# First attention of a hybrid block: one product for the narrow scores, and the next sequence's projections moved within the loop

## The chip, the cores and the metric

The kernel runs on one core of a Trainium2 chip. The metric is the device time of one execution in microseconds. TensorE (PE in the profile) multiplies and transposes, PEld are its weight loads, VectorE is DVE, ScalarE is ACT, GpSimd is POOL, and SyncE (SP) issues the DMAs.

## The reference

A batch of 16 sequences of 512 tokens and width 256 goes through four layers with residuals: attention A, a feed-forward layer with FP4 weights, attention B, and the feed-forward layer again. The change touches attention A and the preparation of weights behind it. Cut to what matters:

```python
q, k, v = split_heads(x @ Wq.T), split_heads(x @ Wk.T), split_heads(x @ Wv.T)   # 16 heads of 16, x normalised
scores = einsum('bhqd,bhkd->bhqk', q, k) * hd ** -0.5
stride = 22                                                                   # int(sqrt(512))
strided = causal & ((i - j < stride) | (j % stride == i % stride))            # heads 0 to 7
fixed = causal & ((j // stride == i // stride) | (j % stride >= stride - 1))  # heads 8 to 15
attn = softmax(where(head_mask, scores, neg_inf))
x = x + (attn @ v) @ Wo.T
```

With the fixed mask a tile of 128 queries needs few keys: its own 128, the 32 before it, and each 22nd key of the whole row (16 "far" columns).

## The kernel before

`attention_a` computes one sequence after another. A sequence has 16 groups n of four heads: `group(n)` gives the half c (0: strided heads, the wide half; 1: fixed heads), the tile t of 128 queries and the parity e. Groups 0 to 7 are wide, with 128, 256, 384 and 512 keys (two groups of each), groups 8 and 9 have 128 keys, groups 10 to 15 are narrow with 176 keys: 16 far and 160 near.

The loop over n is a pipeline that each engine goes through in an order written out by hand. In slot n, for each of the four heads j, TensorE computes the score (`score_head`), transposes the probabilities of group n-1 (`turn_head`, into one of two banks that VectorE and ScalarE empty by turns in `move_turned`), and weighs the values of group n-2 (`weigh`) behind the second head. VectorE masks and takes the maximum (`mask_max`, line 330), ScalarE takes the exponential (`exps`, line 409). A score of head j waits for the maximum of the same head in the group before, since there is one score bank a head.

Beside this, TensorE does one "side job" at the end of some slots (`a_side_jobs`), all in the one PSUM bank `side`: xT0 and xT1 turn the next sequence's normalised input, Q0, K0, V0 and Q1, K1, V1 are its projections for each half, R0 and R1 turn the reciprocal sums, y0 and y1 are the output projection of the sequence before. The result is moved away in slot n+1. xT and V go behind the second head, on one engine. For Q and K ScalarE writes a high part behind the second head (line 396) and VectorE the low part behind the third (line 304), both into `part`; TensorE's next side job waits for the semaphore `s_free` that this gives. SyncE then places the parts with six DMAs for each of Q and K (`place`, line 222) into `stack_q` and `stack_k`, from which the scores are read. `part` is shared by both halves, so ScalarE waits before the high part of one half until all twelve DMAs of the other half have landed:

```python
wait(act, s_placed[1 - c], 192 * (c if s is None else s + 1 + c))
```

The DMAs of half 1 wait for the third group's scores of the next sequence, as `stack_k` of that half is read until then.

Behind the attention, `prepare` quantises three weight matrices in blocks and turns them (`scales`, `mark`, `turn`, `move`), folds the small matrices of attention B (`fold_heads`, `fold_up`, `fold_down`) and runs the first normalised input of the feed-forward layer through its front, all in an order fixed by hand on each engine.

Of the kernel before, what the change touches and what calls it, by code (L numbers as in the profile page):

```python
# [4 lines left out]
FP32 = mybir.dt.float32  # L5
FP16 = mybir.dt.float16
FP32R = mybir.dt.float32r
# [29 lines left out]
A_FAR = 16  # L37
A_REST = A_FAR + A_NEAR
A_NARROW = A_REST + P
A_SIDE_FRONT = ["xT0", "xT1", "Q0", "K0", "V0", "Q1", "K1"]  # L40


# [3 lines left out]
def a_side_jobs(kind):  # L46


    jobs = {}
    if kind != "first":  # L50
        jobs |= {0: "R1", 2: "y0", 3: "y1"}
    if kind != "tail":
        jobs |= {1: "V1", 8: "R0"}
        if kind != "last":
            jobs |= {4: "xT0", 5: "xT1", 6: "Q0", 7: "K0", 9: "V0", 11: "Q1", 13: "K1"}
    return jobs, [jobs[n] for n in sorted(jobs)]


# [12 lines left out]
def attention_a(nc, s_passed, xs, ident, consts, x_in, w_q, w_k, w_v, w_o, masks):  # L71
    front = len(A_SIDE_FRONT)
    ctx = ExitStack()
    with ctx:
# [19 lines left out]
        xT = sb("xT", [P, KC, SEQ])  # L94


        part = sb("part", [P, 2, 2, SEQ], FP32R)
        stack_q = sb("stack_q", [P, 2, 2, 4, SEQ], FP32R)
        stack_k = sb("stack_k", [P, 2, 4, SEQ], FP32R)
        vb = sb("vb", [P, 2, TILES, 4, 64])  # L100
        v_rest = sb("v_rest", [P, TILES - 1, 4, 64])
        probs = sb("probs", [P, 2, 4, SEQ])
# [51 lines left out]
        def chunk(n, row, u):  # L154
# [2 lines left out]
                return row[:, u * P:(u + 1) * P]  # L157
            return row[:, 0:A_REST] if u else row[:, A_REST:A_NARROW]

        def mask_of(n):  # L160
            c, t, _ = group(n)
            if c == 0:
                return mask[:, SEQ - keys(n):SEQ]
            at = SEQ + (P + (t - 1) * A_NARROW if t else 0)
            return mask[:, at:at + keys(n)]
# [32 lines left out]
        def _(sp):  # L198
# [11 lines left out]
            def place(s, job):  # L210

                i, c = "QK".index(job[0]), int(job[1])
                sp.wait_ge(s_free, job_index(s, order_of(s), job) + 1)
                sp.sem_inc(s_passed, 1)
                if s is not None:
                    sp.wait_ge(s_score, 64 * s + (32, 64 + A_AFTER_SWITCH)[c])
                for b, h in enumerate(((0, 0, 1), (0, 1, 0))[i]):
                    for e in range(2):
                        frm = part[64 * e:64 * e + 64, i, h, :].bitcast(FP32)
                        at = slice(64 * e + 16 * b, 64 * e + 16 * b + 16)  # L220
                        to = stack_k[at, c, :, :] if i else stack_q[at, e, c, :, :]
                        sp.dma_start(to.bitcast(FP32), frm).then_inc(s_placed[c], 16)

            def place_all(s):
# [18 lines left out]
            for dst, src in ((wq, w_q), (wk, w_k), (wv, w_v), (wo, w_o), (mask, masks)):  # L243
                sp.dma_start(dst[:], src).then_inc(s_w, 16)
            load(1)
            sp.wait_ge(s_zero, 4)
            place_all(None)
            load(2)
            place_rest(0)
# [9 lines left out]
        @block.gpsimd  # L259
        def _(pool):  # L260
            pool.memset(vb[:], 0.0).then_inc(s_zero, 1)
            pool.memset(stack_q[:].bitcast(FP32), 0.0).then_inc(s_zero, 1)
            pool.memset(stack_k[:].bitcast(FP32), 0.0).then_inc(s_zero, 1)
            pool.memset(v_rest[:], 0.0).then_inc(s_zero, 1)

            def rstd_of(s):
                pool.wait_ge(s_var, s + 1)
                pool.tensor_tensor(out=rstd[:], in0=vare[:], in1=consts[:, 0:TILES],  # L268
                                   op=ALU.pow).then_inc(s_rstd, 1)

            rstd_of(0)
            for s in range(1, SEQS):
                rstd_of(s)

        @block.vector
        def _(dve):
# [20 lines left out]
            def move_side(s, order, job):  # L297
                k = job_index(s, order, job)
                dve.wait_ge(s_job, k + 1)
                c = int(job[-1])  # L300
                if job[0] in "QK":
                    i = "QK".index(job[0])
                    dve.wait_ge(s_hi, parts_before(s, job) + 1)
                    dve.scalar_tensor_tensor(out=part[:, i, 1, :], in0=side[:], scalar=(0.25, 1.0)[i],
                                             in1=part[:, i, 0, :], op0=ALU.mult, op1=ALU.subtract).then_inc(s_free, 1)
                elif job[0] == "V":
                    if s is None and c == 0:
                        dve.wait_ge(s_zero, 1)
                    src = side[:].rearrange("p (a e d) -> p a e d", e=2, d=16)
                    for e in range(2):  # L310
                        dst = vb[:, c, :, :, :].rearrange("p t j d -> p (t j) d")[:, :, 48 * e:48 * e + 16]
                        m = dve.tensor_copy(dst, src[:, :, e, :])
                    m.then_inc(s_free, 1)
                elif job == "xT1":
                    dve.tensor_copy(xT[:, 1, :], side[:]).then_inc(s_free, 1)
                else:
                    for a in range(2):
                        x = x_tile(xs, s - 1, 2 * c + a)
                        m = dve.tensor_tensor(out=x, in0=side[:, a * H:(a + 1) * H], in1=x, op=ALU.add)
                        if a == 1:  # L320
                            m.then_inc(s_free, 1)
# [64 lines left out]
        def _(act):  # L386
            def move_side(s, order, job):
# [5 lines left out]
                elif job[0] in "QK":  # L393
                    i = "QK".index(job[0])
                    wait(act, s_placed[1 - c], 192 * (c if s is None else s + 1 + c))
                    act.activation(part[:, i, 0, :], side[:], ACT.Copy, scale=(0.25, 1.0)[i]).then_inc(s_hi, 1)
                else:
                    s = sequence(s, job)
                    wait(act, s_o, s * 2 + c)
                    act.activation(rsb[:], side[:], ACT.Copy).then_inc(s_rsb, 1)  # L400
                    act.wait_ge(s_rsb, s * 2 + c + 1)
                    act.sem_inc(s_free, 1)
# [35 lines left out]
        def _(pe):  # L438
# [34 lines left out]
            def score_head(s, n, j):  # L473
# [4 lines left out]
                    pe.wait_ge(s_placed[c], 192 * (s + 1))  # L478
                q = stack_q[0:112, e, c, j, t * P:(t + 1) * P]
                if narrow(n):  # L480
                    far = slice(A_STRIDE - 1, A_STRIDE * A_FAR, A_STRIDE)
                    mm(score[j][:, 0:A_FAR], q, stack_k[0:112, c, j, far], start=True, stop=True)
                    m = mm(score[j][:, A_FAR:A_NARROW], q, stack_k[0:112, c, j, t * P - A_NEAR:(t + 1) * P],
                           start=True, stop=True)
                else:
                    m = mm(score[j][:, 0:keys(n)], q, stack_k[0:112, c, j, 0:keys(n)], start=True, stop=True)  # L486
                m.then_inc(s_score, 1)

            def turn_head(s, n, j):
# [82 lines left out]
def prepare(nc, ident, wguT, wdT, a, w, front):  # L572
# [5 lines left out]
    with ctx:  # L578
# [39 lines left out]
        row1 = pb("row1", [P, H])  # L618

        s_raw = [sem("loaded_" + n) for n, *_ in items]  # L620
        s_w = sem("second_attention_loaded")
        s_v = sem("scale_steps")
        s_inv = sem("inverse_ready")
# [14 lines left out]
                    turns.append((m, k, half))  # L638
        for c in range(IC):
            turns.append((2, c, 0))  # L640
        loads = [(wqT, "b_wqT"), (wkT, "b_wkT"), (c2q, "b_c2q"), (bq, "b_bq"), (bk, "b_bk"), (bv, "b_bv"), (bc, "b_bc"),
                 (w1T, "b_w1T"), (wm, "b_wm"), (b1, "b_b1"), (bm, "b_bm"), (wqoT, "b_wqoT"), (bqo, "b_bqo"),
                 (w2, "b_w2"), (wq_in, "b_wq"), (bq_in, "b_bq_turned"), (w["bk"], "b_bk_turned"), (w["wk"], "b_wk"),
                 (w["wv"], "b_wv"), (w["wo"], "b_wo"), (w["rows"], "b_rows"), (w["sum8"], "b_sum8")]

        def shape(i):
            _, p, f, _ = items[i]
# [4 lines left out]
        @block.sync  # L652
        def _(sp):
            for (n, p, f, src), dst, s in zip(items, raw, s_raw):
                sp.dma_start(dst[:], src).then_inc(s, 16)
            for dst, name in loads:
                sp.dma_start(dst[:], a[name]).then_inc(s_w, 16)

        @block.gpsimd
        def _(pool):  # L660
# [13 lines left out]
            front.pool_norm(pool, 0)  # L674
            divide(0)
            divide(1)
            front.pool_divide(pool, 0)
            scale(0)
            pool.wait_ge(s_deq, 2)
            divide(2)  # L680
            scale(1)
            front.pool_scale(pool, 0)
            scale(2)

        @block.vector
        def _(dve):
# [35 lines left out]
            front.vector_norm(dve, 0)  # L722
            scales(0)
            scales(1)
            front.vector_scales(dve, 0)
            mark(0)
            scales(2)
            mark(1)
            front.vector_round(dve, 0)
            for n in range(4):  # L730
                move(n)
            mark(2)
            dve.wait_ge(s_deq, 1)
            for n in range(4, len(turns)):
                move(n)
            dve.wait_ge(s_w, 16 * len(loads))
            dve.tensor_scalar(out=w["wq"][:], in0=wq_in[:], scalar1=CW_SCALE, scalar2=None, op0=ALU.mult)
            dve.tensor_scalar(out=w["bq"][:], in0=bq_in[:], scalar1=CW_SCALE, scalar2=None, op0=ALU.mult)
# [11 lines left out]
        def _(act):  # L750
# [12 lines left out]

            front.scalar_standard(act, 0)
            magnitude(0)
            front.scalar_magnitude(act, 0)
            magnitude(1)
            magnitude(2)
            for n in range(8):
                high(n)  # L770

        @block.tensor
        def _(pe):
# [41 lines left out]
                    m = mm(row2[:], bqo[:, n:n + 1].to_broadcast([P, P]), w2[:, n, :], start=n == 0, stop=n == FC - 1)  # L815
                m.then_inc(s_mm, 1)

            pe.wait_ge(s_w, 16 * len(loads))
            fold_heads()
            for n in range(4):  # L820
                turn(n)
            fold_up()
            for n in range(4, 8):
                turn(n)
            fold_down()
            for n in range(8, len(turns)):
                turn(n)


class XFront:  # L830
# [1328 lines left out]
```

## Time and profile before

| | |
|---|---|
| median of 3 runs | 3564.15 us (3558.09 to 3564.78) |
| profiled execution | 3559.97 us, span in the trace 3558.2 us |
| attention A | from 3.6 us (first memset) to 1060 us |
| preparation | 1060.3 to 1132.9 us |
| a sequence of attention A | 63.2 us |
| busy: PE, DVE, ACT, POOL | 3088.3, 2790.0, 2184.9, 1121.6 us |

Times in the rows are microseconds from the start of the span. "128x176 f32" is partitions by elements. In a row of the timeline the bracket says how long the engine stood idle before it and what released it.

### The profile page before, as it was taken

How to read it: one execution, taken by the hardware profiler on the slowest of the kernel's cores; microseconds unless marked ns; L12 is line 12 of the kernel's file. 1: busy time of each engine (PE TensorE's matmuls, PEld its weight loads, DVE VectorE, ACT ScalarE, POOL GpSimd, SP SyncE). 2: the span in 40 equal slices, each digit the busy share in tenths (PEclk: the TensorE clock that was granted, in tenths of full speed). 3: DMA queues.
4: the chain of work that ended last, by engine and by line, in shares of the span. 5: the costliest groups of instructions: out<-in, count | busy, mean ns of one | idle time of the engine just before them, and what ended most of it. 6: DMA issues, size and time to landing. Idle time of an engine off the chain costs nothing. (4 is left out here: it accounts for less than half of the span.)

```text
span 3558.2 us, 70567 instructions
## 1 busy us (share of the span) xinstructions
PE 3088.3 (87%) x24024; PEld 2396.3 (67%) x24024; DVE 2790.0 (78%) x7209; ACT 2184.9 (61%) x5360; POOL 1121.6 (32%) x664
## 2 busy tenths in 40 slices
PE   6999999999985999995888888888888886799998
PEld 4666666666664888884556556656655654688888
DVE  4776777767767999993778888888888887699997
ACT  3777777777762343432777877777777775344443
POOL 1000000000004555553123444433333333455554
PEclk9999999999996999997898989989999997899999
DMA  4344443434422000001344444334434433111000
GB/s 90 46 70 62 62 71 45 70 62 63 63 37 102 13 19 19 19 19 30 48 61 69 62 72 72 60 60 67 72 60 67 71 54 89 42 36 32 29 30 24
DMA packets 134182, 190.46 MB, mean 54 GB/s; under 512 B 15126, under 2 KB 81558, under 8 KB 133142
## 3 DMA queue, kind: packets, MB, share of 16 engines
q1 hardware_dynamic: 133830, 185.95, 30.3%
q8 instruction: 199, 3.26, 0.4%
q14 instruction: 153, 1.25, 0.2%
HBM read 45.65 MB, written 28.84 MB: 21 GB/s over the span
## 5 line engine op out<-in xcount | busy, mean ns | idle before, releaser
L409 ACT ACTIVATE a_probs<-a_probs,a_negmax 128x176 f32<-128x176 f32 (+4 forms) x1024 | 502.6, 491 | 265.7 <-DVE a_negmax L330 259.8
L330 DVE CUSTOM_DVE_ANT_0 a_probs<-a_mask,a_score 128x176 f32<-128x176 f32 (+4 forms) x1024 | 404.1, 401 | 270.5 <-PE a_score L486 114.4
L1718 DVE CUSTOM_DVE_ANT_0 b_u<-b_u,b_score 128x512 f32<-128x512 f32 x512 | 340.8, 682 | 135.3 <-PE b_score L1973 132.8
L494 PE MATMUL a_turned<-ident,a_probs 128*128 128x128 f32 (+1 forms) x2176 | 411.4, 280 | 37.7 <-DVE a_pT L339 29.7
L1843 ACT ACTIVATE b_u<-b_u,b_negmax 128x512 f32<-128x512 f32 x512 | 367.1, 717 | 112.0 <-DVE b_negmax L1718 110.4
L1247 PE MATMUL f_y_bank<-f_wdT,f_hqT 128*128 128x256 f32 x1536 | 357.0, 382 | 40.6 <-ACT f_hqT L1186 36.9
L1710 DVE SCALAR_TENSOR_TENSOR b_u<-b_u,b_score 128x1024 f32<-128x1024 f32 x256 | 310.0, 1215 | 93.5 <-ACT b_u L1836 91.1
L1836 ACT ACTIVATE b_u<-b_score 128x1024 f32<-128x1024 f32 x256 | 262.0, 1024 | 162.3 <-PE b_score L1963 161.9
L1247 PEld LDWEIGHTS f_y_bank<-f_wdT,f_hqT 128*128 128x128 f32 x1536 | 284.6, 190 | 89.5 <-issue 56.4
L1982 PE MATMUL b_turned<-ident,b_u 128*128 128x128 f32 x2048 | 320.6, 281 | 24.9 <-DVE b_pT L1724 19.5
L1982 PEld LDWEIGHTS b_turned<-ident,b_u 128*128 128x128 f32 x2048 | 248.6, 145 | 97.1 <-issue 59.9
L1179 ACT ACTIVATE f_h_mag<-f_hu 128x704 f32<-128x704 f32 x128 | 100.9, 788 | 342.7 <-POOL f_hu L1062 342.7
L1070 POOL TENSOR_TENSOR f_hq<-f_h_mark,f_nscale 128x704 f32<-128x704 f32 x128 | 177.6, 1388 | 404.3 <-DVE f_h_mark L1128 404.3
L268 POOL TENSOR_TENSOR a_rstd<-a_vare,consts 128x4 f32<-128x4 f32 x16 | 16.1, 1008 | 908.7 <-DVE a_vare L286 908.6
L494 PEld LDWEIGHTS a_turned<-ident,a_probs 128*128 128x128 f32 (+1 forms) x2176 | 236.4, 134 | 94.5 <-issue 51.7
L1973 PE MATMUL b_score<-b_stack 96*128 96x512 f32 x512 | 272.1, 546 | 20.1 <-DVE b_u L1710 20.0
L1230 PE MATMUL f_gate<-f_wguT,f_xqT 128*128 128x352 f32 x1536 | 283.6, 334 | 0.0
L1230 PE MATMUL f_up<-f_wguT,f_xqT 128*128 128x352 f32 x1536 | 277.3, 329 | 0.0
L486 PE MATMUL a_score<-a_stack_k,a_stack_q 112*128 112x128 f32 (+3 forms) x640 | 248.8, 403 | 1.1 <-DVE a_negmax L330 1.1
L1230 PEld LDWEIGHTS f_gate<-f_wguT,f_xqT 128*128 128x128 f32 x1536 | 249.5, 193 | 0.1
L1230 PEld LDWEIGHTS f_up<-f_wguT,f_xqT 128*128 128x128 f32 x1536 | 244.6, 189 | 0.0
L339 DVE COPY a_pT<-a_turned 128x256 f32<-128x256 f32 (+3 forms) x512 | 224.0, 438 | 4.9 <-PE a_turned L494 1.1
(236 smaller groups left out, 7132.1 us busy)
## 6 DMA issues: line engine op xcount, KB each, us to landing
b_stack<-b_part SPq DMA_DIRECT2D x192, 256.0 KB, 8.2
a_stack_q<-a_part SPq DMA_DIRECT2D x192, 128.0 KB, 4.3
a_stack_k<-a_part SPq DMA_DIRECT2D x192, 128.0 KB, 5.3
xs<-in_x_dram SPq DMA_DIRECT2D x16, 512.0 KB, 8.5
x_before_b<-xs SPq DMA_DIRECT2D x16, 512.0 KB, 2.9
b_xin<-x_before_b SPq DMA_DIRECT2D x16, 512.0 KB, 12.2
b_xres<-x_before_b SPq DMA_DIRECT2D x16, 512.0 KB, 3.9
x_after_b<-b_xres SPq DMA_DIRECT2D x16, 512.0 KB, 5.8
```

What stands on the lines that cost most here:

```text
L330: dve.tensor_tensor_reduce(out=probs[:, n % 2, j, 0:keys(n)], in0=mask_of(n), in1=score[j][:, 0:keys(n)], scale=-1.0, scalar=3.0e38, op0=A ...
L409: act.activation(probs[:, n % 2, j, 0:keys(n)], probs[:, n % 2, j, 0:keys(n)], ACT.Exp, bias=negmax[:, n, j:j + 1], scale=-1.0, accum_out= ...
L486: m = mm(score[j][:, 0:keys(n)], q, stack_k[0:112, c, j, 0:keys(n)], start=True, stop=True)
L494: m = nc.tensor.transpose(turned[j % 2][0:rows, u, :], chunk(n, probs[:, n % 2, j, :], u), ident[:])
L1230: m = mm(dst[:, a, 0:HALF], xqT[:, i, k, t * P:(t + 1) * P], wguT[:, j, k, at:at + HALF], start=p == 0, stop=p == len(products) - 1)
L1247: m = mm(y_bank[:, 0:H], hqT[:, t % 2, c * P:(c + 1) * P], wdT[:, c, :], start=c == 0, stop=c == IC - 1)
L1710: dve.scalar_tensor_tensor(out=u[:, g, d, :], in0=u[:, g, d, :], scalar=10.0, in1=score[:, d, :], op0=ALU.add, op1=ALU.mult).then_inc(s_u, 1)
L1718: dve.tensor_tensor_reduce(out=u[:, n, j, :], in0=u[:, n, j, :], in1=score[:, j, :], scale=-0.05, scalar=3.0e38, op0=ALU.add, op1=ALU.min, ...
L1836: act.activation(u[:, g, d, :], score[:, d, :], ACT.Sin, scale=PI_IN).then_inc(s_sin, 1)
L1843: act.activation(u[:, n, j, :], u[:, n, j, :], ACT.Exp, bias=negmax[:, n, j:j + 1], scale=-1.0, accum_out=sums[:, c, t, j:j + 1]).then_inc ...
L1973: mm(score[:, j, :], stack[0:96, 0, c, j, t * P:(t + 1) * P], stack[0:96, 1, c, j, :], start=True, stop=True).then_inc(s_score, 1)
L1982: m = nc.tensor.transpose(turned[j % 2][:, t, :], u[:, n, j, t * P:(t + 1) * P], ident[:])
```

## The change

Three things are changed. The narrow score becomes one product of 176 columns instead of one of 16 and one of 160: K1's parts are laid out with 176 columns for each of the three narrow tiles (`A_WIDE` = 656 columns), by copying the far and near columns as they are moved out of the bank (three pieces on ScalarE and three on VectorE), and `stack_k` of half 1 becomes `wide_k`. The side jobs xT0, xT1, Q0, K0, V0 and Q1 move from slots 4, 5, 6, 7, 9 and 11 to 6, 7, 9, 10, 11 and 12; K1 stays in 13, R0 in 8. In `prepare` the loads of the heads' fold get their own semaphore and come first, and the orders of all engines are changed: the first input's scales and rounding come behind the weights, `fold_down` behind all turns.

```diff
+A_WIDE = P + (TILES - 1) * A_NARROW
...
-            jobs |= {4: "xT0", 5: "xT1", 6: "Q0", 7: "K0", 9: "V0", 11: "Q1", 13: "K1"}
+            jobs |= {6: "xT0", 7: "xT1", 9: "Q0", 10: "K0", 11: "V0", 12: "Q1", 13: "K1"}
...
-        part = sb("part", [P, 2, 2, SEQ], FP32R)
+        part = sb("part", [P, 2, 2, A_WIDE], FP32R)
-        stack_k = sb("stack_k", [P, 2, 4, SEQ], FP32R)
+        stack_k = sb("stack_k", [P, 4, SEQ], FP32R)
+        wide_k = sb("wide_k", [P, 4, A_WIDE], FP32R)
...
+        def part_pieces(job, row):
+            if job != "K1":
+                return [row[:, 0:SEQ]]
+            blocks = row[:, P:A_WIDE].rearrange("p (t w) -> p t w", w=A_NARROW)
+            return [row[:, 0:P], blocks[:, :, 0:A_FAR], blocks[:, :, A_FAR:A_NARROW]]
+        def side_pieces(job):
+            if job != "K1":
+                return [side[:]]
+            far = side[:, A_STRIDE - 1:A_STRIDE * A_FAR:A_STRIDE].unsqueeze(1).to_broadcast([P, TILES - 1, A_FAR])
+            return [side[:, 0:P], far, near_columns()]
...
-                        to = stack_k[at, c, :, :] if i else stack_q[at, e, c, :, :]
+                        to = (wide_k if c else stack_k)[at, :, :] if i else stack_q[at, e, c, :, :]
...
+            pool.memset(wide_k[:].bitcast(FP32), 0.0).then_inc(s_zero, 1)
...
-                    act.activation(part[:, i, 0, :], side[:], ACT.Copy, scale=(0.25, 1.0)[i]).then_inc(s_hi, 1)
+                    for high, src in zip(part_pieces(job, part[:, i, 0, :]), side_pieces(job)):
+                        m = act.activation(high, src, ACT.Copy, scale=(0.25, 1.0)[i])
+                    m.then_inc(s_hi, 1)
...
-                    far = slice(A_STRIDE - 1, A_STRIDE * A_FAR, A_STRIDE)
-                    mm(score[j][:, 0:A_FAR], q, stack_k[0:112, c, j, far], start=True, stop=True)
-                    m = mm(score[j][:, A_FAR:A_NARROW], q, stack_k[0:112, c, j, t * P - A_NEAR:(t + 1) * P],
+                    at = P + (t - 1) * A_NARROW
+                    m = mm(score[j][:, 0:A_NARROW], q, wide_k[0:112, j, at:at + A_NARROW], start=True, stop=True)
...
             front.vector_norm(dve, 0)
             scales(0)
             scales(1)
-            front.vector_scales(dve, 0)
             mark(0)
             scales(2)
             mark(1)
-            front.vector_round(dve, 0)
             for n in range(4):
                 move(n)
             mark(2)
+            front.vector_scales(dve, 0)
+            for n in range(4, 8):
+                move(n)
             dve.wait_ge(s_deq, 1)
-            for n in range(4, len(turns)):
+            for n in range(8, len(turns)):
                 move(n)
+            front.vector_round(dve, 0)
...
-            pe.wait_ge(s_w, 16 * len(loads))
+            pe.wait_ge(s_heads, 16 * len(head_loads))
             fold_heads()
             for n in range(4):
                 turn(n)
+            pe.wait_ge(s_w, 16 * len(loads))
             fold_up()
-            for n in range(4, 8):
+            for n in range(4, len(turns)):
                 turn(n)
             fold_down()
-            for n in range(8, len(turns)):
-                turn(n)
```

VectorE's low part is cut into the same pieces. In the other engines' orders of `prepare`, GpSimd's division and scaling of the first input move behind the third matrix, and ScalarE writes high parts between the magnitudes.

## Rows read from the trace of the kernel before

**Rows 1.** The page, busy time (share of the span) and instructions of each engine

```profile
PE 3088.3 (87%) x24024; PEld 2396.3 (67%) x24024; DVE 2790.0 (78%) x7209; ACT 2184.9 (61%) x5360; POOL 1121.6 (32%) x664
```

**Rows 2.** Timeline of TensorE's products in sequence 3: start, duration, instruction

```profile
249.28 0.53 PE L486 MATMUL a_score<-a_stack_k,a_stack_q 112*128 112x384 f32 x1
...
250.94 0.45 PE L486 MATMUL a_score<-a_stack_k,a_stack_q 112*128 112x384 f32 x1
...
266.62 1.98 PE L453 MATMUL a_side<-a_xT,a_wk 128*128 128x512 f32 x4 [1.05 <-DVE a_part L304]
...
274.73 0.33 PE L486 MATMUL a_score<-a_stack_k,a_stack_q 112*128 112x128 f32 x1
...
277.47 0.26 PE L482 MATMUL a_score<-a_stack_k,a_stack_q 112*128 112x16 f32 x1
...
283.67 0.58 PE L482 MATMUL a_score<-a_stack_k,a_stack_q 112*128 112x16 f32 x1
...
290.75 0.58 PE L482 MATMUL a_score<-a_stack_k,a_stack_q 112*128 112x16 f32 x1
...
291.49 0.26 PE L482 MATMUL a_score<-a_stack_k,a_stack_q 112*128 112x16 f32 x1
291.60 0.33 PE L483 MATMUL a_score<-a_stack_k,a_stack_q 112*128 112x160 f32 x1
291.76 0.39 PE L494 MATMUL a_turned<-ident,a_probs 128*128 128x128 f32 x2
...
296.44 0.31 PE L486 MATMUL a_score<-a_stack_k,a_stack_q 112*128 112x128 f32 x1
```

**Rows 3.** Timeline of TensorE in sequence 15, the last

```profile
1010.09 0.45 PE L486 MATMUL a_score<-a_stack_k,a_stack_q 112*128 112x384 f32 x1
...
1029.53 0.33 PE L486 MATMUL a_score<-a_stack_k,a_stack_q 112*128 112x128 f32 x1
...
1032.69 0.26 PE L482 MATMUL a_score<-a_stack_k,a_stack_q 112*128 112x16 f32 x1
...
1040.49 0.26 PE L482 MATMUL a_score<-a_stack_k,a_stack_q 112*128 112x16 f32 x1
```

**Rows 4.** Groups by line and shape, 0 to 1100 us: busy, mean ns | idle before

```profile
L453 PE MATMUL a_side<-a_xT,a_wk 128*128 128x512 f32 x128 | 65.3, 635 | 23.6 <-DVE a_part L304 23.6
L339 DVE COPY a_pT<-a_turned 128x128 f32<-128x128 f32 x128 | 36.7, 287 | 0.1
L462 PE MATMUL a_side<-ident,a_rec 128*128 128x128 f32 x128 | 20.0, 279 | 13.2 <-DVE a_part L304 13.2
```

**Rows 5.** Timelines of ScalarE and VectorE in slot 12 of sequence 3

```profile
286.15 0.58 ACT L396 ACTIVATE a_part<-a_side 128x512 fp32r<-128x512 f32 x1
...
286.84 0.69 DVE L304 SCALAR_TENSOR_TENSOR a_part<-a_side,a_part 128x512 fp32r<-128x512 f32 x1
```

**Rows 6.** Timeline at the start of the attention, before the first scores

```profile
26.25 3.88 SPq L222 DMA_DIRECT2D a_stack_q<-a_part  x6
...
31.31 3.75 SPq L222 DMA_DIRECT2D a_stack_k<-a_part  x6
...
41.02 0.60 ACT L396 ACTIVATE a_part<-a_side 128x512 fp32r<-128x512 f32 x1 [10.60 <-DMA a_stack_k<-a_part]
```

**Rows 7.** Timelines of VectorE and TensorE in the preparation

```profile
1097.58 1.21 DVE L921 SCALAR_TENSOR_TENSOR f_x_mark<-f_x_mag,f_xu 128x1024 f32<-128x1024 f32 x1
1098.82 4.58 DVE L924 SCALAR_TENSOR_TENSOR f_x_mark<-f_x_mag,f_x_mark 128x1024 f32<-128x1024 f32 x1
...
1103.99 1.41 PE L783 MATMUL w_bank<-ident,w_raw_gate 88*128 88x88 f32 x8 [11.69 <-DVE f_wguT L716]
...
1123.71 3.72 PE L815 MATMUL w_row<-w_w,w_bqo 128*128 128x256 f32 x16
```

**Rows 8.** Windows: busy of each engine in a stretch, granted clock, DMA share, GB/s

```profile
236.00:299.00 63.00, 58.20 (x577) 43.38 (x576) 45.64 (x192) 46.36 (x167) 1.01 (x1) 1.00 0.41 62
...
1033.00:1035.00 2.00, 1.99 (x15) 1.15 (x14) 1.39 (x8) 1.76 (x9) 0.00 (x0) 0.50 0.03 8
```

More of the change, by code:

```diff
@@ L158, in chunk, with near_columns @@
             return row[:, 0:A_REST] if u else row[:, A_REST:A_NARROW]
+        def part_pieces(job, row):
[8 more added lines that the diff above has]
+            return [side[:, 0:P], far, near_columns()]
+        def near_columns():
+            near = side[:, P - A_NEAR:2 * P]
+            return bass.AP(near.tensor, near.offset, [list(near.ap[0]), [P, TILES - 1], [1, P + A_NEAR]])
         def mask_of(n):
@@ L218, in place @@
                     for e in range(2):
-                        frm = part[64 * e:64 * e + 64, i, h, :].bitcast(FP32)
+                        frm = part[64 * e:64 * e + 64, i, h, 0:(A_WIDE if job == "K1" else SEQ)].bitcast(FP32)
                         at = slice(64 * e + 16 * b, 64 * e + 16 * b + 16)
-                        to = stack_k[at, c, :, :] if i else stack_q[at, e, c, :, :]
+                        to = (wide_k if c else stack_k)[at, :, :] if i else stack_q[at, e, c, :, :]
                         sp.dma_start(to.bitcast(FP32), frm).then_inc(s_placed[c], 16)
@@ L245, in _ @@
             load(1)
-            sp.wait_ge(s_zero, 4)
+            sp.wait_ge(s_zero, 5)
             place_all(None)
@@ L303, in move_side @@
                     dve.wait_ge(s_hi, parts_before(s, job) + 1)
-                    dve.scalar_tensor_tensor(out=part[:, i, 1, :], in0=side[:], scalar=(0.25, 1.0)[i],
-                                             in1=part[:, i, 0, :], op0=ALU.mult, op1=ALU.subtract).then_inc(s_free, 1)
+                    for low, high, src in zip(part_pieces(job, part[:, i, 1, :]), part_pieces(job, part[:, i, 0, :]),
+                                              side_pieces(job)):
+                        m = dve.scalar_tensor_tensor(out=low, in0=src, scalar=(0.25, 1.0)[i], in1=high,
+                                                     op0=ALU.mult, op1=ALU.subtract)
+                    m.then_inc(s_free, 1)
                 elif job[0] == "V":
@@ L480, in score_head @@
                 if narrow(n):
-                    far = slice(A_STRIDE - 1, A_STRIDE * A_FAR, A_STRIDE)
-                    mm(score[j][:, 0:A_FAR], q, stack_k[0:112, c, j, far], start=True, stop=True)
-                    m = mm(score[j][:, A_FAR:A_NARROW], q, stack_k[0:112, c, j, t * P - A_NEAR:(t + 1) * P],
+                    at = P + (t - 1) * A_NARROW
+                    m = mm(score[j][:, 0:A_NARROW], q, wide_k[0:112, j, at:at + A_NARROW], start=True, stop=True)
+                else:
+                    m = mm(score[j][:, 0:keys(n)], q, (wide_k if c else stack_k)[0:112, j, 0:keys(n)],
                            start=True, stop=True)
-                else:
-                    m = mm(score[j][:, 0:keys(n)], q, stack_k[0:112, c, j, 0:keys(n)], start=True, stop=True)
                 m.then_inc(s_score, 1)
@@ L620, in prepare @@
         s_raw = [sem("loaded_" + n) for n, *_ in items]
+        s_heads = sem("head_weights_loaded")
         s_w = sem("second_attention_loaded")
@@ L640, in prepare @@
             turns.append((2, c, 0))
[L641 to L644, printed above, removed]
+        head_loads = [(wqT, "b_wqT"), (wkT, "b_wkT"), (c2q, "b_c2q"), (bq, "b_bq"), (bk, "b_bk"), (bv, "b_bv"),
+                      (w["wo"], "b_wo")]
+        loads = [(w1T, "b_w1T"), (wm, "b_wm"), (b1, "b_b1"), (wqoT, "b_wqoT"), (bqo, "b_bqo"), (w2, "b_w2"),
+                 (bc, "b_bc"), (bm, "b_bm"), (wq_in, "b_wq"), (bq_in, "b_bq_turned"), (w["bk"], "b_bk_turned"),
+                 (w["wk"], "b_wk"), (w["wv"], "b_wv"), (w["rows"], "b_rows"), (w["sum8"], "b_sum8")]
         def shape(i):
@@ L655, in _ @@
                 sp.dma_start(dst[:], src).then_inc(s, 16)
+            for dst, name in head_loads:
+                sp.dma_start(dst[:], a[name]).then_inc(s_heads, 16)
             for dst, name in loads:
@@ L676, in _ @@
             divide(1)
-            front.pool_divide(pool, 0)
             scale(0)
@@ L681, in _ @@
             scale(1)
+            scale(2)
+            front.pool_divide(pool, 0)
             front.pool_scale(pool, 0)
-            scale(2)
         @block.vector
@@ L732, in _ @@
             mark(2)
+            front.vector_scales(dve, 0)
+            for n in range(4, 8):
+                move(n)
             dve.wait_ge(s_deq, 1)
-            for n in range(4, len(turns)):
+            for n in range(8, len(turns)):
                 move(n)
+            front.vector_round(dve, 0)
+            dve.wait_ge(s_heads, 16 * len(head_loads))
             dve.wait_ge(s_w, 16 * len(loads))
@@ L765, in _ @@
             magnitude(0)
+            magnitude(1)
+            for n in range(4):
+                high(n)
+            magnitude(2)
+            for n in range(4, 8):
+                high(n)
             front.scalar_magnitude(act, 0)
[L767 to L770, printed above, removed]
         @block.tensor
```

## The prediction

> **What bounds the kernel now.** I read the page first: TensorE is the busiest engine at 87% [rows 1], but that is an average over stages. The change touches only the first attention (to 1060 us) and the preparation of the weights behind it (to 1132.9 us). The chain that ended last lies wholly in the last stage and says nothing of these, so I went to the timeline of one sequence in the steady part (sequence 3), engine by engine. Its pattern repeats: the third score of group 4 starts at 250.94 there and at 1010.09 twelve sequences later [rows 2, 3], 63.26 us each.
>
> A "slot" is the pass over one group n of four heads. By the first score of each group on TensorE, slots 4 to 9 take 277.47-249.28=28.19 us, slots 10 and 11 6.20, slots 12 and 13 7.08, slots 14 and 15 5.69 [rows 2]. Three things are to be seen.
> First, in the narrow half a slot takes 2.85 us (14, 15), and one with a Q or K projection about 4.2 (7.08 less 2.85), its TensorE time of 1.3 to 1.4 on top: there the projection delays the next group in full, but nothing waits for a bank.
> Second, all side jobs share one PSUM bank. The job of slot n is moved away in slot n+1: ScalarE writes the high part behind its second exponential, VectorE the low part behind its third maximum, and only then may TensorE issue another job. Where two jobs follow each other TensorE stands, as K0 does at 266.62 for the low part of Q0 [rows 2]; over the stage K projections waited 23.6 us so, and R jobs 13.2 [rows 4].
> Third, the last sequence makes no projections for a next one, and its slots 4 to 9 show what the wide half costs without them: third score of group 4 to third score of group 9 is 1029.53-1010.09=19.44 us, in sequence 3 it is 274.73-250.94=23.79 [rows 2, 3].
>
> **Part 1, the merged score.** Each narrow head loses a product of 16 columns and widens one from 160 to 176. Start to start the first takes 0.11 us and the second 0.16 (291.49, 291.60, 291.76) [rows 2]; in proportion 176 columns take less than 0.18, and I take 0.165. So 0.105 us of TensorE per head, 24 heads a sequence, 16 sequences: 40 us if TensorE's work alone set the pace. Between slots without a job it does not: the pace is a ring of one third score, its maximum, its exponential, ScalarE's move, a transpose, the weighing and the next third score, and it holds one score of the four. I take 0.1 us a slot there and keep 0.42 for a rival. The price is that K1 is moved in three pieces (128, 48 and 480 columns). The 512-column forms take 0.58 and 0.69 us [rows 5], a 128-column move of VectorE 0.29 [rows 4], so about 0.15 is fixed and 1.05 ns a column: three pieces of 656 columns cost VectorE 0.35 more and ScalarE about 0.25. They sit in slot 14 within that ring: +0.2 for the slot, bounds 0 and 0.6. K1's transfers grow by 28%, run in slots 2 to 5, and slot 8 is their first reader: nothing. The wider memset and K1 at the start: at most 1 us once, I take 0.9.
>
> **Part 2, wide half.** Slots 4 and 5 lose both transposes of the input, 6 and 7 get them for Q0 and K0, 9 gets Q0 for V0. I take 19.44 us from third score 4 to third score 9 by the last sequence; the two transposes (0.41 us each) should fall into the waits that its ring leaves. Slot 4 starts 1.66 before that stretch, slot 10 now starts 2.74 behind it and will start 1.95 behind (Q0 is 0.5 shorter than V0, and R0 is released earlier): 23.05 us against 28.19. Gain 5.1; bounds 4.0, if the transposes and their moves add in full, and 5.3.
>
> **Part 2, narrow half.** Now Q0, K0, V0, Q1, K1 follow each other in slots 9 to 13. The price of such a step stands in slot 12: first score 283.67, high part of Q1 286.15 to 286.73, low part 286.84 to 287.53 [rows 2, 5]: 3.86 us after the group's first score; one product fewer on the way makes it 3.74, with 0.05 to the next job. Counted from the start of slot 10 (its heads have 128 columns behind them, 0.1 less): K0 starts at 3.7 and takes 1.32, slot 11 starts at 5.0, V0 at 8.75 (1.79), slot 12 at 10.55; V0 is moved at the second head already, so Q1 starts at 12.75 and slot 13 at 14.05. Q1's high part would be due at 16.4.
> What is late next is a transfer. ScalarE may write Q1's high part only when all twelve transfers of Q0 and K0 have landed. Now that is hidden: nothing waits for them in sequence 3. After the change Q0's begin at 3.65 and K0's 5 us later. Just that spacing stands at the start of the stage: Q0's at 26.25, K0's at 31.31, and ScalarE, after a wait of 10.60 us, goes on at 41.02 [rows 6], 14.77 us after the first. So the part is written at 3.65+14.77=18.4, 2.0 us late; bounds 1.2 (if the wider spacing of a steady sequence frees the queues sooner) and 2.0. Behind it on ScalarE wait two exponentials of group 13 and a move, and for these the transposes of slot 14. K1 starts at 18.4+0.58+0.1+0.69+0.05=19.85, slot 14 at 21.15. Now slots 10 to 13 take 13.28: +7.9.
>
> **Attention in sum.** -5.1+7.9, +0.2 for the pieces and -0.2 for slots 14 and 15: +2.8 us for each of the 15 sequences that prepare a next one, +42. The last has only the merged scores, -0.7. Start +0.9.
>
> **Part 3, preparation.** VectorE rounds the first normalised input (1.2 and 4.58 us) before it moves the turned weights, and TensorE waits 11.69 us, to 1103.99 [rows 7]. In the new order this comes behind the moves: 5.8 earlier. The input's scales leave the path too, but GpSimd's products hold up the marks: 2.4 more. Against it the second fold, whose last third starts at 1123.71 and takes 3.72 us, is now TensorE's last work, with VectorE's closing copies (2 us) behind it rather than beside the turns: 1.9 back. -6.3 us, bounds -2 (the copies and a fold at half clock) and -9. The fold of the heads, allowed earlier by its own loads, gains nothing: the first turn waits for GpSimd.
>
> 3559.97+42-0.7+0.9-6.3=3595.9. The profiled execution is 4 us below the median of the runs, within their spread; I predict 3596.
>
> **The rivals.**
> *The move gives what TensorE's work alone would allow (0.16).* Were the bank and the transfers no limit, slots 10, 12 and 13 would take 4.2-0.44=3.76, slot 11 4.23, slots 14 and 15 2.8 each: 21.1 us against 18.97. With 5.1 won before it that is -3.0 a sequence, 3560-45-6=3509. For it: TensorE does not stop behind Q1 and K1 now. Against it: both places where such jobs touch show the wait. It decides at 24.5 us from the start of slot 10 to the next sequence: below, the kernel is faster; I count 26.9.
> *The transfers land in time (0.15).* The bank waits stay: +0.8 a sequence, 3560+12-6=3566, no change.
> *The clock falls in each sequence (0.19).* In sequence 3 the granted clock is 1.00; in the last one, with more gaps, it is 0.50 (1.2 GHz) in the stretch from 1033 to 1035 [rows 8], and slots 11 and 12 take 1040.49-1032.69=7.80 us [rows 3], about 1.6 more than they should. After the change TensorE stands four times in slots 10 to 13, for 7 of 21 us. At 1.6 to 3 us (projections at half clock) 15 times: 3620 to 3641.
> The Trainium skill ("TensorE: Matmul & The Clock Gate", HAM oscillation) tells of a kernel that fell back to the slow clock in every tile because TensorE waited for transfers in each. The trace agrees in the last sequence alone; by that rule this rival would be the forecast.
>
> **How the numbers follow.** My forecast has 0.50 and its own range is 3580 to 3612, from the bounds above. With the second and the third rival the range is 3562 to 3640; it leaves out the first. A measurement of this kernel can tell a change of about 0.2% (7 us) from none. Faster 0.17, same 0.11, slower 0.72.
>
> **What would show it.** A period of 66 us in the middle sequences; TensorE idle before K0, V0 and K1 with the low part as releaser, 1.5 to 2 us or more each time; ScalarE idle before Q1's high part with a transfer as releaser, 15 times; no such wait in slots 7 and 8; the preparation 6 us shorter. I am wrong if the jobs of slots 10 and 11 start without a wait, if third score 4 to 9 stays above 21 us, or if the clock falls.

## The result, and the profile after

The changed kernel takes 3623.74 us (median of 4 runs, 3623.35 to 3624.51) against 3563.18 us for the kernel before (3558.09 to 3564.78). The ratio is 1.0177, with a 95% interval of 1.0160 to 1.0193: slower. The profiled execution has a span of 3621.6 us, 63.4 more than before.

The page says little: TensorE has 384 products fewer and is busy 18 us longer (compare [rows 1]). There is less work, but more of it runs at half clock, as is shown below.

```profile
PE 3106.1 (86%) x23640; PEld 2373.9 (66%) x23640; DVE 2794.7 (77%) x7241; ACT 2184.0 (60%) x5392; POOL 1118.8 (31%) x665
```

The timeline of TensorE in sequence 3, and the third score of group 4 in sequence 15 (start, duration, instruction; in the bracket the idle time before it and what ended it):

```profile
264.13 0.53 PE L511 MATMUL a_score<-a_stack_k,a_stack_q 112*128 112x384 f32 x1
...
265.78 0.45 PE L511 MATMUL a_score<-a_stack_k,a_stack_q 112*128 112x384 f32 x1
...
285.23 0.33 PE L511 MATMUL a_score<-a_wide_k,a_stack_q 112*128 112x128 f32 x1
...
287.50 0.65 PE L509 MATMUL a_score<-a_wide_k,a_stack_q 112*128 112x176 f32 x1
...
291.20 1.99 PE L480 MATMUL a_side<-a_xT,a_wk 128*128 128x512 f32 x4 [1.32 <-DVE a_part L328]
...
296.44 2.05 PE L484 MATMUL a_side<-a_wv,a_xT 128*128 128x128 f32 x16 [1.21 <-DVE a_part L328]
...
300.44 1.98 PE L480 MATMUL a_side<-a_xT,a_wq 128*128 128x512 f32 x4
...
307.41 3.38 PE L480 MATMUL a_side<-a_xT,a_wk 128*128 128x512 f32 x4 [2.93 <-DVE a_part L328]
...
309.80 1.14 PE L509 MATMUL a_score<-a_wide_k,a_stack_q 112*128 112x176 f32 x1
...
316.38 0.31 PE L511 MATMUL a_score<-a_stack_k,a_stack_q 112*128 112x128 f32 x1
...
1082.65 0.44 PE L511 MATMUL a_score<-a_stack_k,a_stack_q 112*128 112x384 f32 x1
```

From sequence 3 to 15 it is (1082.65-265.78)/12=68.07 us each, where it was 63.26 [rows 2, 3]. Fifteen times 4.81 is 72. By slots, in sequence 3: 4 to 9 take 287.50-264.13=23.37 us (28.19 before), 10 to 13 take 309.80-287.50=22.30 (13.28), 14 and 15 take 6.58 (5.69). Three jobs stand behind a wait for VectorE's low part. The last, K1, waits 2.93 us and then takes 309.80-307.41=2.39 us to the next score where Q0, V0 or K0 at full clock take 1.4 to 1.8.

What is late ahead of it stands in the timelines of SyncE, ScalarE and VectorE:

```profile
291.24 3.84 SPq L243 DMA_DIRECT2D a_stack_q<-a_part  x6
296.47 3.77 SPq L243 DMA_DIRECT2D a_stack_k<-a_part  x6
```

```profile
305.95 0.60 ACT L422 ACTIVATE a_part<-a_side 128x512 fp32r<-128x512 f32 x1 [1.62 <-DMA a_stack_k<-a_part]
```

```profile
306.66 0.69 DVE L328 SCALAR_TENSOR_TENSOR a_part<-a_side,a_part 128x512 fp32r<-128x512 f32 x1 [1.86 <-ACT a_part L422]
```

Twelve transfers land 14.71 us behind the first issue (14.77 at the start of the stage [rows 6]), ScalarE waits 1.62 us for them, VectorE for ScalarE, TensorE for VectorE. And here is what came on top; the windows give start and end, length, busy time of PE, PEld, DVE, ACT and POOL, the granted clock, DMA share and GB/s:

```profile
306.00:308.00 2.00, 0.59 (x1) 0.30 (x2) 0.94 (x3) 1.61 (x6) 0.00 (x0) 0.96 0.00 0
308.00:310.00 2.00, 2.00 (x5) 0.94 (x3) 0.00 (x0) 0.17 (x2) 0.00 (x0) 0.50 0.04 8
310.00:312.00 2.00, 2.00 (x23) 1.21 (x22) 0.85 (x4) 0.47 (x3) 0.00 (x0) 0.69 0.00 0
```

The granted clock falls to 0.50 of full speed (1.2 GHz) while K1 runs. I summed the granted clock over windows of 3 us from 46 to 1006 us: 3.9 us at half clock before, 84.4 us now. Of these 9.3 us lie at the start of the stage and the rest in 18 stretches; a 19th follows at 1041.7. In the 15 sequences that prepare a next one it fell eleven times in K1 or in the wait just ahead of it, seven times in K0 and once in V0 (twice in some sequences). One sequence, whose K1 starts at 650.37, was spared: it took 66.43 us. Two in which it fell in K0 alone took 66.59 and 66.57 us: Q1's part waits for the transfers anyway, and what K0 lost shortened that wait. The later falls, in K1 above all, cost time: sequences with one took 67.5 to 70.3 us. The waits of the whole steady part (engine, tile, line, releaser: us in total, times, longest):

```profile
PE a_side L480 <- DVE a_part L328: 55.1, 30, 3.1
PE a_side L484 <- DVE a_part L328: 17.7, 15, 1.2
ACT a_part L422 <- DMA a_stack_k<-a_part: 15.6, 14, 1.8
```

Before, K projections waited 15.8 us and R jobs 13.2 in the same stretch; the wait of R0 is gone, as foreseen, and nothing waits in slots 7 and 8.

The preparation, from the first load of the weights to the issue that stores them, fell from 72.56 to 67.63 us; SyncE's and TensorE's timelines:

```profile
1130.72 0.35 SPq L683 DMA_DIRECT2D w_raw_gate<-in_w_gate_dram  x1
...
1198.35 0.33 SPq L1075 DMA_DIRECT2D kept_gu<-f_wguT  x1
```

```profile
1158.38 1.44 PE L818 MATMUL w_bank<-ident,w_raw_gate 88*128 88x88 f32 x8 [5.63 <-POOL w_raw_gate L700]
...
1166.68 1.41 PE L818 MATMUL w_bank<-ident,w_raw_gate 88*128 88x88 f32 x8 [6.86 <-DVE f_wguT L746]
...
1186.06 6.49 PE L848 MATMUL w_down<-w_w,w_wqoT 128*8 128x256 f32 x16
1192.48 3.72 PE L850 MATMUL w_row<-w_w,w_bqo 128*128 128x256 f32 x16
```

The wait of 11.69 us [rows 7] is 6.86 now, and the second fold stands at the end.

### The profile page after: what moved, and what is told of

Read it like the earlier page. It is cut to its first block and busy times, and to the rows that moved or that the text cites. A ratio compares the mean times of both kernels' runs of the same rounds, so it can differ in the third digit from the quotient of the medians.

```text
span 3621.6 us, 69866 instructions
## 1 busy us (share of the span) xinstructions
PE 3106.1 (86%) x23640; PEld 2373.9 (66%) x23640; DVE 2794.7 (77%) x7241; ACT 2184.0 (60%) x5392; POOL 1118.8 (31%) x665
## 5 line engine op out<-in xcount | busy, mean ns | idle before, releaser
L2016 PE MATMUL b_turned<-ident,b_u 128*128 128x128 f32 x2048 | 319.5, 281 | 21.0 <-DVE b_pT L1758 15.8
L1997 PE MATMUL b_score<-b_units 96*128 96x512 f16 x512 | 161.5, 398 | 64.8 <-DVE b_u L1744 52.1
```

Source lines behind the costliest of these rows:

```text
L2016: m = nc.tensor.transpose(turned[j % 2][:, t, :], u[:, n, j, t * P:(t + 1) * P], ident[:])
```

## The experiments

Twelve kernels ran. "Period" is the distance of the third scores of group 4 from sequence 3 to 15, divided by 12; "half clock" is the sum of above, of which 2 to 11 us lie at the start of the stage, before 64 us. Both come from the one profiled execution, while "us" is the median of 4 to 10. The two can differ: the profiled execution of e4 is the slowest of five (3554.15 us), that of e8 the fastest of six (3569.92 us), those of e7 and e11 the slowest of theirs. Each ratio is against the kernel before on the same chip.

| run | us | ratio (95%) | period | half clock |
|---|---|---|---|---|
| before | 3563.18 | 1 | 63.26 | 3.9 |
| after | 3623.74 | 1.0177 (1.0160 to 1.0193) | 68.07 | 84.4 |
| e1 merged score alone | 3559.33 | 0.9993 (0.9984 to 1.0002) | 63.13 | 10.9 |
| e2 job slots alone | 3623.41 | 1.0181 (1.0162 to 1.0199) | 67.49 | 63.1 |
| e3 preparation alone | 3554.05 | 0.9979 (0.9969 to 0.9990) | 63.27 | 8.7 |
| e4 jobs spaced | 3539.75 | 0.9947 (0.9929 to 0.9965) | 62.82 | 31.9 |
| e5 slots of before | 3554.33 | 0.9980 (0.9971 to 0.9990) | 63.13 | 4.6 |
| e6 two part buffers | 3580.94 | 1.0053 (1.0035 to 1.0072) | 65.08 | 12.2 |
| e7 six products ahead of K1 | 3648.30 | 1.0233 (1.0205 to 1.0261) | 69.43 | 37.0 |
| e8 earlier release | 3585.92 | 1.0063 (1.0044 to 1.0082) | 65.09 | 33.9 |
| e9 three products ahead of K1 | 3616.50 | 1.0153 (1.0133 to 1.0173) | 67.14 | 31.3 |
| e10 spaced, two buffers | 3538.87 | 0.9933 (0.9914 to 0.9953) | 62.55 | 25.9 |
| e11 old slots, two buffers | 3547.26 | 0.9955 (0.9938 to 0.9972) | 63.14 | 2.6 |
| e12 products ahead of K0, V0, K1 | 3605.25 | 1.0118 (1.0103 to 1.0133) | 66.57 | 6.9 |

### The parts one by one: e1, e2, e3, e5

e1 is the kernel before with `wide_k`, the pieces and the merged score; e2 the kernel before with the line of the slots changed and nothing else; e3 the kernel before with the new `prepare`; e5 the changed kernel with

```diff
-            jobs |= {6: "xT0", 7: "xT1", 9: "Q0", 10: "K0", 11: "V0", 12: "Q1", 13: "K1"}
+            jobs |= {4: "xT0", 5: "xT1", 6: "Q0", 7: "K0", 9: "V0", 11: "Q1", 13: "K1"}
```

> Only the merged narrow score (one product of 176 columns, K1 moved in three pieces); side jobs and preparation as before. My theory (moving the jobs is the loss): faster than before by a little. In each of the 16 sequences slots 12, 14, 15 gain 0.1 us each, slots 10, 11 and 13 up to 0.4 us, K1's pieces cost 0.2: about -1 us a sequence, -16 us in all, 3547 us. Rival (the merged score or its pieces are the loss): slower than before, 3580 us or more.

> Only the side jobs in their new slots; two products a narrow head and preparation as before. My theory: the whole loss is here, +4 to +5 us a sequence, 3625 to 3640 us, ScalarE waits 1 to 1.5 us for the transfers before Q1's high part in 14 sequences, TensorE before K0, V0 and K1, and the granted clock falls to 0.50 once a sequence. Rival: less than +10 us.

> Only the new order of the preparation. My theory: -4 us (the block took 72.9 us before and about 69 after), 3560 us, all of it between the end of the attention and the first turn of the feed-forward layer; the first attention keeps 63.2 us a sequence. Rival: the half clock during the folds gives it back, no change.

> The changed kernel with the side jobs back in their old slots (merged score and new preparation stay). If the three parts add, 3559.3-3561.7-8 from the single runs: about 3552 us, the whole loss gone. If the parts act on each other (the merged score pays only where TensorE is loaded, in the new slots), more than 3560 us.

The whole loss is in e2, the one line of slots, and e5 takes it away again. e3 shortens the block by 4.6 us (1058.18 to 1126.13 is 67.95); its ratio stands for 7.5 us, with an interval from 3.6 to 11, and no row shows where more than the 4.6 would come from. The merged score gives less than I expected of it: the time moved by 2 us, within its interval, where I had expected 16. In the new slots it gives nothing that shows either: e2, without it, has a period of 67.49, the changed kernel 68.07, with more time at half clock. In sequence 3 of e1:

```profile
279.23 0.33 PE L509 MATMUL a_score<-a_wide_k,a_stack_q 112*128 112x176 f32 x1
...
292.08 0.65 PE L509 MATMUL a_score<-a_wide_k,a_stack_q 112*128 112x176 f32 x1
...
298.19 0.31 PE L511 MATMUL a_score<-a_stack_k,a_stack_q 112*128 112x128 f32 x1
```

```profile
294.46 0.82 ACT L422 ACTIVATE a_part<-a_side 128x128 fp32r<-128x128 f32 x3
```

```profile
295.39 0.97 DVE L328 SCALAR_TENSOR_TENSOR a_part<-a_side,a_part 128x128 fp32r<-128x128 f32 x3 [0.37 <-ACT a_part L422]
```

Slots 10 to 13 take 12.85 us (13.28 before), 0.1 less a slot; slots 14 and 15 take 6.11 (5.69), 0.4 more. The second and third fence show K1's three pieces, in slot 14's ring: 0.82 us on ScalarE for 0.58 before, 0.97 on VectorE for 0.69 [rows 5]. These 0.52 us are the likely reason why the gain is given back; no run has the pieces without the merged score.

### The transfers taken away: e6

A `part` buffer for each half, so that Q1 never waits for the transfers of Q0 and K0:

```diff
-        part = sb("part", [P, 2, 2, A_WIDE], FP32R)
+        part = [sb("part", [P, 2, 2, SEQ], FP32R), sb("part1", [P, 2, 2, A_WIDE], FP32R)]
...
-                    wait(act, s_placed[1 - c], 192 * (c if s is None else s + 1 + c))
+                    wait(act, s_placed[c], 0 if s is None else 192 * (s + 1))
```

> The changed kernel with a part buffer for each half, so that Q1's high part waits for no transfer of Q0 and K0; slots as changed. The bank waits before K0, V0 and K1 stay. My theory: ScalarE's wait of 1.1 to 1.6 us goes, TensorE's wait before K1 falls from 2.9 to about 1.3 us, with it most of the falls of the clock: 1.5 to 3 us a sequence, 3580 to 3600 us. Rival (only the bank matters): above 3615 us.

The waits of e6 in the same stretch, none of ScalarE for a transfer among them:

```profile
PE a_side L480 <- DVE a_part L328: 37.9, 30, 1.3
PE a_side L484 <- DVE a_part L328: 17.7, 15, 1.2
```

K1 waits 1.21 us there, slots 10 to 13 of sequence 3 take 19.60 us, and nearly all of the half-clock time has gone with the long wait (12.2 us are left of 84.4). Also the first third score of group 4 comes at 56.19 instead of 62.65: the 10.60 us of [rows 6] were the same wait, paid once at the start.

### The bank released earlier: e8

e6 with the high part of Q and K behind the first exponential and the low part behind the second maximum, so that the next job could start a head earlier.

> As the version with two part buffers, and for Q and K ScalarE writes the high part behind the first exponential and VectorE the low part behind the second maximum, one head earlier each: the bank is free about 0.7 us sooner. My theory: TensorE's waits before K0, V0 and K1 shrink from 1.3 to 0.6 us each, 2 us a sequence or 30 us below the version with two part buffers. Rival (the earlier moves delay the next exponential and maximum by as much): no gain.

```profile
DVE a_part L328 <- ACT a_part L422: 54.7, 60, 1.2
PE a_side L482 <- DVE a_part L328: 25.3, 30, 0.9
PE a_side L486 <- DVE a_part L328: 12.2, 15, 1.1
```

TensorE waits 18 us less than in e6, but VectorE now stands 54.7 us for ScalarE (19.1 in e6) in front of the maxima that the scores need. Most of the wait changed its place, and the time did not fall. The rival that I named is not the only reason: in the profiled execution the clock fell in nine sequences of e8, each time from slot 14 or 15 on, against three of e6. Where it held, five of six sequences took 64.3 to 64.5 us, against 64.7 to 65.1 in e6, so the earlier release won some 0.4 us a sequence, and lost it again where the clock fell.

### What the clock takes: e7, e9, e12

Products that nobody reads, into a score bank that is already free, fill the waits of TensorE. In e9:

```diff
+                    if jobs.get(n) == "K1":
+                        pe.wait_ge(s_mask, s * 64 + 4 * n + 1)
+                        for _ in range(3):
+                            mm(score[0][:], wk[:, 0, 0:P], xT[:, 0, :], start=True, stop=True)
```

e7 has six of them, e12 these three and one each ahead of K0 and V0.

> The changed kernel with six products of 512 columns that nobody reads (into the first score bank, free by then) on TensorE just before K1, where it stands for 2.9 us. They add work but no wait. My theory (the clock falls because TensorE stands there): the granted clock stays at 1.00 in that slot and behind it, K1 takes 1.4 us instead of 2.4, 1.2 us or so a sequence: 3600 to 3608 us. Rival (the wait alone costs, the clock does not): same as the changed kernel, 3624 us, or slower.

> The changed kernel with three unread products of 512 columns ahead of K1 in slot 13, 2.65 us of TensorE by the run with six (which took 5.32 us), so they fit in the wait of about 3 us and cost nothing by themselves. It leaves nothing out of the computation. If the half clock that K1 and slot 14 run at comes from TensorE's standing ahead of K1, K1 takes 1.3 us instead of 2.6 to 3.4, slot 14 is some 1 us shorter, and the total is 3600 to 3612. If the clock falls for the gaps of slots 10 to 12 all the same, it moves to another slot and the total stays at 3618 to 3630.

> The run with three unread products ahead of K1, and one more (0.9 us) ahead of K0 and one ahead of V0, inside the waits of 1.32 and 1.21 us. Nothing is left out of the computation. In the run with three the clock still fell in 7 sequences, each time within K0 or V0, the first job behind such a wait, and the sequences in which it did not fall took 66.2 to 66.7 us. If the waits are what lets the clock fall, it stays up, the period is 66.3 to 66.6 in the mean, K0 and V0 start no later, and the total is 3600 to 3607: what the clock took is then 1.5 to 1.7 us a sequence. If the falls have another cause they stay at 7 or so, the total at 3612 to 3620.

e7 was mis-sized. I had taken a product of 512 columns for 0.4 us; it is recorded as two, and takes 0.9:

```profile
312.85 5.32 PE L554 MATMUL a_score<-a_xT,a_wk 128*128 128x512 f32 x12
...
318.00 1.88 PE L480 MATMUL a_side<-a_xT,a_wk 128*128 128x512 f32 x4
```

Six overshot the wait by 2.4 us, and the run (3648 us, where I had forecast 3600 to 3608) says nothing of the time that the clock takes, only that K1 ran at full clock behind them. Of e9, its sequence 2:

```profile
222.05 1.98 PE L480 MATMUL a_side<-a_xT,a_wk 128*128 128x512 f32 x4 [1.32 <-DVE a_part L328]
...
227.28 3.55 PE L484 MATMUL a_side<-a_wv,a_xT 128*128 128x128 f32 x16 [1.21 <-DVE a_part L328]
```

K1 kept its clock in every sequence, but in eight of the 15 it fell in K0 or V0, the first or second job behind a wait, as in this V0 of 3.55 us. The first seven of them are the ones that the next expectation counts. By the times e9 can't be told from the changed kernel (the intervals overlap). e12 fills these gaps too. Its sequence 3:

```profile
283.67 0.65 PE L509 MATMUL a_score<-a_wide_k,a_stack_q 112*128 112x176 f32 x1
...
285.89 1.02 PE L554 MATMUL a_score<-a_xT,a_wk 128*128 128x512 f32 x2
287.37 1.99 PE L480 MATMUL a_side<-a_xT,a_wk 128*128 128x512 f32 x4 [0.46 <-DVE a_part L328]
...
300.48 2.74 PE L554 MATMUL a_score<-a_xT,a_wk 128*128 128x512 f32 x6
303.45 1.98 PE L480 MATMUL a_side<-a_xT,a_wk 128*128 128x512 f32 x4 [0.23 <-DVE a_part L328]
304.87 0.65 PE L509 MATMUL a_score<-a_wide_k,a_stack_q 112*128 112x176 f32 x1
...
310.96 0.31 PE L511 MATMUL a_score<-a_stack_k,a_stack_q 112*128 112x128 f32 x1
```

TensorE does five products more in each sequence (4.78 us of work), and the ratio falls from 1.0177 to 1.0118, with intervals apart: the clock is at half for 6.9 us instead of 84.4, all of it at the start, before 57 us, and slots 10 to 13 take 304.87-283.67=21.20 us. This is the wait for the transfers and the bank without the clock. The period of 66.57 agrees with the one spared sequence of the changed kernel, 66.43; one sequence of 68.36 us, longer by a stall in its wide half, is in it, and the others take 66.4 in the mean.

### A better order: e4, e10, e11

e4 changes the one line of slots again, so that no Q, K or V follows another without a slot between, except where the second head's move makes it harmless (V0, then Q1):

```diff
-            jobs |= {6: "xT0", 7: "xT1", 9: "Q0", 10: "K0", 11: "V0", 12: "Q1", 13: "K1"}
+            jobs |= {4: "xT0", 5: "xT1", 6: "Q0", 9: "K0", 11: "V0", 12: "Q1", 14: "K1"}
```

e10 is e4 with e6's two buffers, e11 the slots of before with them.

> The changed kernel with the jobs spaced so that no Q or K projection has another job behind it: xT0 4, xT1 5, Q0 6, R0 8, K0 9, V0 11, Q1 12, K1 14. My theory (the loss is the wait for the bank behind a projection, and through it the transfers and the clock): TensorE waits for no low part any more, ScalarE for no transfer, the clock stays at 1.00, and a sequence takes 60 to 61 us against 63.2 before: about 3515 us, faster than both kernels. Rival (late projections in the narrow half are bad wherever they stand): about 3564 us or slower.

> The changed kernel with the jobs spaced as in the run that was 0.5% faster than before (4 xT0, 5 xT1, 6 Q0, 8 R0, 9 K0, 11 V0, 12 Q1, 14 K1) and with a part buffer for each half. In the steady sequences no wait for a transfer is left in the spaced order, so there the second buffer gives nothing; at the start of the stage it took the wait for the transfers ahead of Q1's high part, worth 6 us. Expected 3534, range 3526 to 3541. If the buffer gives nothing here, 3540; if the earlier start of half 1's parts lets the clock fall more often, up to 3548.

> The changed kernel with the job slots of before (4, 5, 6, 7, 9, 11, 13) and a part buffer for each half. It tells the start from the order: with the slots of before no sequence waits for a transfer, so only the start can gain. Expected 3548 (the run with the old slots and one buffer took 3554.33, less 6 at the start), period still 63.16; rival: the second buffer also shortens a sequence, 3540 or less; no gain at all, 3554.

e4 and e10 beat both kernels, by 0.5% and 0.7% against before, and can't be told apart from each other. That is less than the 1.4% that I had expected of e4. With one buffer the spaced order beats the old one (e5), with intervals apart; with two (e10 and e11) the intervals overlap. In e4 TensorE waits for a low part once after 44 us, at the start of the stage, and a sequence in which the clock holds takes 61.5 to 62.3 us, not 60 to 61. The clock does not hold in each: in sequence 3 it fell at 275.9 with no job waiting.

```profile
271.00:274.00 3.00, 2.82 (x22) 1.65 (x21) 1.35 (x8) 1.70 (x8) 0.00 (x0) 1.00 0.00 0
274.00:277.00 3.00, 2.40 (x19) 1.58 (x18) 2.46 (x11) 2.50 (x12) 0.00 (x0) 0.82 0.14 49
277.00:280.00 3.00, 3.00 (x19) 3.00 (x18) 0.35 (x3) 1.14 (x5) 0.00 (x0) 0.61 1.07 147
```

By my estimate from 62.82 less 61.85, fifteen times, this costs some 15 us over the stage in the profiled execution; it was the slowest of five, and the others may have lost less. What makes the clock fall there stays open. e11's median is 7 us below e5's, near what I expected, though the intervals just touch. In its trace the first third score of group 4 comes 6 us earlier and the period is that of e5, so the gain is at the start.

## Why the prediction was right, and where it was short

The sign and the place were right, and so was the mechanism of the two waits, for the bank and for the transfers. But the time is 28 us above the number I gave. It lies outside the forecast's own range (3580 to 3612) and within that of the third rival (3620 to 3641), which I gave 0.19; only the wide range, which covers both, holds it. And one of my own signs of being wrong came: the clock fell. Point by point:

**Wide half.** Right. Third score of group 4 to third score of group 9 is 285.23-265.78=19.45 us, as the last sequence had it (19.44); the transposes fell into waits. Slots 4 to 9 take 23.37 us for the 23.05 of the sum.

**Narrow half.** Right, once the clock is held: 21.20 us in e12 against 21.15. In sequence 3 Q1's high part is written 305.95-287.50=18.45 us behind the start of slot 10, where I had 18.4. The waits ahead of K0 and V0 were 1.32 and 1.21 us each sequence ("1.5 to 2 us or more" was a little high). ScalarE waited for the transfers 14 times, 1.1 us in the mean and 1.8 at most; in e12, where the clock holds, 15 times and 22.1 us, 1.5 each. I had taken 2.0 with bounds of 1.2 and 2.0.

**The clock, the step that failed.** I made it a rival of 0.19, at 1.6 to 3 us a sequence, instead of a term of the sum, which so put it at nothing. Evidence stood in my own text: in the last sequence, which has gaps of the kind that the change puts into every one, the clock already fell to 0.50 [rows 8]. It was the evidence of one execution: in e3, whose attention is that of the kernel before, the last sequence kept its clock. e12 against the changed kernel is 68.07-66.57=1.50 us a sequence, 22 us in all, and 0.59% in the ratios, 21 us; the rival's lower edge, 1.6, was close. The Trainium skill ("TensorE: Matmul & The Clock Gate", HAM oscillation) tells of a kernel that fell back to the slow clock in every tile because TensorE waited for transfers in each; the trace agrees in the main, with 19 stretches at half clock in the 15 sequences that prepare a next one, though one sequence was spared.

**Slots 14 and 15.** I had them unchanged (+0.2 for the pieces, -0.2 for the scores). In e1 they take 0.42 more, so if the scores gave their 0.2, the pieces cost about 0.6, the top of their bounds. My figures for one piece were not added up rightly either: two more times 0.15 and 144 columns of 1.05 ns are 0.45 us on VectorE, not 0.35; the trace of e1 has 0.28. With 0.1 less a slot before, the merged score gives 0.13 us a sequence, and in e1 a time that can't be told from before. It saved TensorE's work in a place where the ring sets the pace.

**Preparation.** -4.9 for -6.3, within the bounds. The fold behind the turns runs partly at half clock, and longer than before: the products for `w_down` take 6.49 us, 5.09 before.

**The rivals.** "TensorE's work alone" fell to the waits, as argued; "the transfers land in time" to the 15.6 us of ScalarE.

So the loss has these terms, by period, 15 times: the order with its bank waits, less the gain of the wide half, 65.08-63.26=1.8 us (27 us, e6, with 12 us at half clock left in it), the transfers 66.57-65.08=1.5 us (22 us), the clock 1.5 us (22 us); against them stands the preparation with 5. The sum is 66, the spans differ by 63.4: the start took 1.2 us more, and against it stand the last sequence, 2.2 us shorter (the clock held there this time), and 2.0 us in the stages behind, which the change does not touch. The first two terms are 49 us, where I had 42. That they add this way is taken from one run for each and not tested in every combination.

## What to carry to other kernels

A job that moves from a half with idle time into a half where its result must pass three engines before the next may start costs the chain of these engines, not its own time; here, spacing the jobs by a slot took the loss away and a little more (e4). A part buffer shared by two stages of a pipeline costs nothing as long as the transfers are far apart, and has to be costed again when the stages move together. And where a change adds gaps on TensorE to each turn of a loop (1.2 to 3.1 us here), the clock belongs in the sum if any turn with such gaps already shows it; unread products in the gaps are a way to measure what it takes.

## What the runs showed of the hardware

The granted clock fell behind short waits, and not each time. In eight of 15 sequences of e9 it fell in K0 or V0, behind waits of 1.32 or 1.32 and 1.21 us, and in others with the same two waits it did not. In e6 each sequence has these two waits and a third of 1.21 us, and it fell in three of 15. Around K1, with a wait of 1.8 to 3.1 us ahead of it, it fell in eleven sequences of the changed kernel, and in one with 2.72 us and one with 1.92 it held. In e4 it fell (to 0.61 in the mean of a window) where TensorE was busy for 2.82, 2.40 and 3.00 of 3 us. No run here tells what decides between a fall and none.
